# Moving ScalarE's K and V copies behind the second score's exps in a decoder block on one Trainium2 core

## The chip, the cores and the metric

The kernel runs on one core of a Trainium2 chip. The metric is device time in microseconds (us), the median of several executions; lower is better. Engines are called as in the profile: PE (matmul) with its weight loads PEld, DVE (VectorE), ACT (ScalarE), POOL (GpSimd), SP (which only issues DMAs here).

## What is computed

A decoder layer with three residual steps, each followed by a layer norm: linear attention over x (32 batches of 56 tokens, width 128, 16 heads), cross attention of x to a context of 1500 keys per batch, and a small feed-forward. Cut to what matters here, the cross attention:

```
qh = heads(q @ Wq.T + bq)          # 16 heads of 8
kh = heads(k @ Wk.T + bk)          # k = v = ctx, (32, 1500, 128)
vh = heads(v @ Wv.T + bv)
scores = einsum('bhqd,bhkd->bhqk', qh, kh) / sqrt(8)
attn = softmax(scores, axis=-1)
out = einsum('bhqk,bhkd->bhqd', attn, vh)
return concat(out) @ Wo.T + bo
```

## The kernel before

A front part does the linear attention and the queries of all 32 batches, a last part the feed-forward. Between them, from about 131 to 704 us, lies the main loop over batches, unrolled by two: `u` = 0 and 1. Each engine has its own written order of work; semaphores join them.

**Scores.** A batch has 12 scores of 125 keys (`KT`). Score t is 8 matmuls (line 1066) into two of three PSUM banks used in turn (`scores`). ACT turns each bank into probabilities with one `exp` activation (line 756), so a score has a pair of exps. PE may begin score t once the first exp of score t-1 is done. The products of probabilities and values, `pv`, are 32 short matmuls each time two scores are taken up (lines 1083 and 1089); they come two scores late.

**Steps and units.** A batch is six steps m of two scores. Between the scores PE does units of work for batches b+1 and b+2, in the order that `PLAN` writes out by hand:

```
PLAN = ((("M1", "M1", "M1", "K2"), ("M1", "M1"), ()),
        (("M1", "M1", "V"), ("M1", "M1"), ("T",)),
        (("M1", "K2", "M1", "M1"), (), ("M1", "M1")),
        (("K2", "Z"), (), ("X",)),
        (("M2", "V"), ("M2", "M2"), ("Y",)),
        (("M2", "M2", "V", "M2", "M2"), (), ()))
```

Each step has three parts, called one, two and three in the code. PE's order within a step is score 2m, part one, score 2m+1, part two, the `pv` of two earlier scores, part three. K2 (a third of the key projection of batch b+2, three matmuls, line 954) and V (a third of the values of batch b+1, twelve short matmuls, line 962) are copied out by ACT (`k_copy`, line 776, and `v_copy`, line 765). The M units (line 974) are a pass of scores from which DVE takes row maxima (line 1313); M1 is for batch b+1, M2 for b+2. X turns the maxima over and ACT copies them to `mT` (`m_copy`, line 771), which SP then brings into `q_diag` with four DMAs. T, Z and Y finish the output of a pair of batches and come in u=0 alone; DVE takes them up.

**The ring.** Every unit takes the next of four PSUM banks (`ring`), in the order of `PLAN`; a unit waits in `release` until the unit four places earlier has been taken out by its engine, through `DONE` (`k32_done` and `v_done` for K and V). Certain M units go as pairs (`PAIRS`): PE waits for the banks of both before the first. Counting units of u=0 from zero, K2's first (3) shares a bank with an M of step 1 (7), V's first (8) with an M of step 2 (12), K2's second (13) with the last M of step 2 (17), K2's third (18) with V's second (22), this with an M of step 5 (26), and V's third (28) with the second M of the next batch's step 0. Round u=1 is 28 units long and turned by three banks: V's first shares with K2's second, K2's third with an M of step 4's part two, the others follow as in u=0. I write K0, K1, K2 and V0, V1, V2 for the three units and copies of a batch, N0 to N6 for its M2 units.

**Other queues.** POOL splits the context in two halves, casts each copied K third to `kh` (line 580) and takes the rest `kl`; SP stores both halves and loads them back, stacked, as `k_stack` (line 439). SP's order in a batch is: load `k_stack`, place the maxima, load context, store K halves.

Of the kernel before, what the change touches and what calls it, by code (L numbers as in the profile page):

```python
# [241 lines left out]
def decoder_block(nc, ctx_dram, x_dram, pack_dram, out_dram, m):  # L242
# [6 lines left out]
    with ExitStack() as stack:  # L249
# [124 lines left out]
        with nc.Block() as block:  # L374
# [330 lines left out]
            def _(act):  # L705
# [44 lines left out]
                def exp(b, t):  # L750
                    for half in range(2):
                        k = 2 * t + half
                        act.wait_ge(s_ready, b * 2 * KT + k + 1)
                        if half == 0:
                            wait_past(act, pv_done, b * KT + t - PBUF + 1)
                        nc.scalar.activation(probs[0:KP, t % PBUF, half * 2 * GC:(half + 1) * 2 * GC],  # L756
                                             scores[k % RING_AT][0:KP, 0:2 * GC], ACT.Exp, scale=SCALE).then_inc(p_ready, 1)

                def v_copy(n, i, u, bank):
                    act.wait_ge(ready["V"], n * 3 + i + 1)  # L760
                    if i == 0:
                        wait_past(act, pv_done, (n - 1) * KT)
                    at = 4 * i * G * VW + 8
                    to = v_ext[u][0:KP, at:at + 4 * G * VW].rearrange("p (x a c) -> p x a c", a=2, c=VW // 2)
                    nc.scalar.copy(to[:, :, :, 0:2 * HD],  # L765
                                   bank[0:KP, :].rearrange("p (x a c) -> p x a c", a=2, c=2 * HD)).then_inc(v_done, 1)

                def m_copy(n, bank):
                    act.wait_ge(ready["X"], n + 1)
                    wait_past(act, m_placed, n * 64)  # L770
                    nc.scalar.copy(mT[:, :], bank.bitcast(F16)[0:MB, 0:P]).then_inc(m_ready, 1)  # L771

                def k_copy(n, i, bank):
                    act.wait_ge(ready["K"], n * KC + i + 1)
                    wait_past(act, kl_done, (n - 1) * KC + i + 1)
                    nc.scalar.activation(k32[:, i * CH:(i + 1) * CH], bank[:, 0:CH], ACT.Identity,  # L776
                                         bias=w("bk")).then_inc(k32_done, 1)
# [28 lines left out]
                def body(b, u, s1, s2):  # L806

                    def copies(units):
                        for kind, i in units:
                            bank = ring[slots[u][kind, i]]  # L810
                            if kind == "V" and s2:
                                v_copy(b + 1, i, 1 - u, bank)
                            if kind == "X" and s2:
                                m_copy(b + 1, bank)
                            if kind == "K1" and s2:
                                k_copy(b + 1, i, bank)
                            if kind == "K2" and s1:
                                k_copy(b + 2, i, bank)

                    for m, (one, two, three) in enumerate(plans[u]):  # L820
                        exp(b, 2 * m)
                        if not s2 and 2 * m in X2T_STEPS:
                            x2_T(X2T_STEPS.index(2 * m))
                        copies(one)
                        exp(b, 2 * m + 1)
                        copies(two + three)

                def x2_T(q):
                    act.wait_ge(x2T_ps, q + 1)
                    nc.scalar.copy(x2T[:, q, :], X2T_BANK).then_inc(x2T_sb, 1)  # L830

                for b in range(2):
                    body(b, b % 2, True, True)
                with act.Fori(1, B // 2 - 1) as i:
                    for u in range(2):
                        body(i * 2 + u, u, True, True)
                body(B - 2, 0, False, True)
                body(B - 1, 1, False, False)

# [705 lines left out]
```

## Time and profile before

| what | us |
|---|---|
| median of three runs | 758.32 |
| lowest and highest | 755.79 and 760.76 |
| profiled execution, its own time | 758.05 |
| span of that execution in the trace | 756.3 |

The profiled execution is one more run of the same program, with the hardware profiler on; its mean granted TensorE clock is 0.965 of full speed. All durations come from it. Times of rows count from the start of its span.

### The profile page before, as it was taken

To read this page: it belongs to the slowest core of one execution; us is meant where nothing else is said; L and a number is where in the kernel's file an instruction comes from. 1 tells how busy PE (TensorE), PEld (TensorE's weight loads), DVE (VectorE), ACT (ScalarE), POOL (GpSimd) and SP (SyncE) were. 2 spreads that over 40 slices of the span, in tenths; PEclk is the share of its full clock that TensorE was granted. 3 is DMA by queue.
4 is the path that set the end of the run, shared out by engine and by line. 5 is a ranking of instruction groups with operands and counts; after the bars stand their busy time and mean duration, and the time that the engine had idled before them with its cause. 6 is when DMAs were issued, how large, how long until landed. Compare 5 with 4: busy or idle time off the path is not lost.

```text
span 756.3 us, 33186 instructions
## 1 busy us (share of the span) xinstructions
PE 677.2 (90%) x12468; PEld 436.8 (58%) x12468; DVE 585.3 (77%) x1139; ACT 549.2 (73%) x1123; POOL 471.1 (62%) x507
## 2 busy tenths in 40 slices
PE   6779864989799999999999999999999999997883
PEld 3456431555566666666666666666666666665552
DVE  5768966766678888888888878888888788884597
ACT  4537523876678888888888888888888888887751
POOL 6525524574657677777777677767777767623464
PEclk9989976999999999999999999999999999999997
DMA  7203503587667777877788877778777778760001
GB/s 215 82 2 101 87 15 83 80 187 139 128 136 142 144 156 156 174 158 147 147 158 150 153 148 152 147 143 154 156 168 166 148 142 161 132 108 11 1 1 49
DMA packets 39405, 93.20 MB, mean 123 GB/s; under 512 B 7880, under 2 KB 14536, under 8 KB 39368
## 3 DMA queue, kind: packets, MB, share of 16 engines
q1 hardware_dynamic: 39368, 92.69, 60.6%
q8 instruction: 25, 0.41, 0.3%
q14 instruction: 12, 0.10, 0.1%
HBM read 66.06 MB, written 26.54 MB: 122 GB/s over the span
## 4 chain that ended last, share of the span: by engine, by line
PE 65%; DVE 14%; issue 9%; ACT 7%; DMA 2%; SPq 1%; POOL 1%; ACTq 0%; DVEq 0%; POOLq 0%
PE psum L974 13%; PE psum L1066 12%; PE psum L1083 11%; PE psum L962 9%; PE psum L1089 8%; DVE mx L1313 4%; ACT probs L756 4%; PE psum L954 3%; PE psum L905 2%; DMA q_diag<-mT 1%; PE psum L891 1%; DVE rden L1241 1%; PE psum L982 1%; DVE k_stack L1452 1%; DVE kf L1210 1%
## 5 line engine op out<-in xcount | busy, mean ns | idle before, releaser
L1313 DVE TENSOR_REDUCE mx<-psum 128x1 f32<-128x500 f32 x672 | 422.1, 673 | 103.3 <-PE psum L974 100.1
L756 ACT ACTIVATE probs<-psum 125x448 f32<-125x448 f32 x768 | 376.3, 544 | 88.8 <-PE psum L1066 85.2
L974 PE MATMUL psum<-kh,q_max 64*128 64x500 f16 (+1 forms) x672 | 148.6, 383 | 12.4 <-DVE mx L1313 11.2
L1066 PE MATMUL psum<-q_diag,k_stack 64*128 64x112 f16 x3072 | 143.0, 212 | 11.3 <-ACT probs L756 2.6
L1083 PE MATMUL psum<-probs,v_ext 125*32 125x112 f32 x3072 | 149.8, 266 | 2.0 <-issue 2.0
L1089 PE MATMUL psum<-probs,v_ext 125*32 125x112 f32 x3072 | 145.3, 261 | 0.0
L580 POOL CAST kh<-k 128x500 f16<-128x500 f32 x96 | 57.7, 601 | 134.5 <-ACT k L776 126.7
L1066 PEld LDWEIGHTS psum<-q_diag,k_stack 64*128 64x128 f16 x3072 | 90.3, 95 | 82.7 <-ACT probs L756 49.7
L568 POOL TENSOR_TENSOR c_hl<-c_in,c_hl 128x500 f16<-128x500 f32 x96 | 110.4, 1150 | 7.7
L586 POOL TENSOR_TENSOR kl<-k,kh 128x500 f16<-128x500 f32 x96 | 107.2, 1145 | 0.0
L1083 PEld LDWEIGHTS psum<-probs,v_ext 125*32 125x32 f32 x3072 | 74.3, 109 | 32.7 <-issue 23.7
L1089 PEld LDWEIGHTS psum<-probs,v_ext 125*32 125x32 f32 x3072 | 87.7, 111 | 0.0
L566 POOL CAST c_hl<-c_in 128x500 f16<-128x500 f32 x96 | 59.4, 619 | 38.9 <-PE psum L962 36.1
L962 PE MATMUL psum<-WvH,c_hl 128*128 128x128 f16 x768 | 76.7, 222 | 4.5 <-issue 4.5
L974 PEld LDWEIGHTS psum<-kh,q_max 64*128 64x128 f16 (+1 forms) x672 | 38.3, 94 | 69.7 <-DVE mx L1313 31.1
L962 PEld LDWEIGHTS psum<-WvH,c_hl 128*128 128x128 f16 x768 | 58.4, 99 | 24.9 <-DVE mx L1313 11.4
L776 ACT ACTIVATE k<-psum,pack 128x500 f32<-128x500 f32 x96 | 65.1, 679 | 9.6 <-PE psum L954 8.2
L962 PE MATMUL psum<-WvL,c_hl 128*128 128x128 f16 x384 | 70.4, 221 | 0.0
L765 ACT COPY v_ext<-psum 125x512 f32<-125x512 f32 x96 | 56.4, 588 | 5.9 <-PE psum L962 5.8
L954 PE MATMUL psum<-c_hl,WkH 128*128 128x500 f16 x192 | 57.2, 380 | 0.3 <-ACT mT L771 0.3
L607 POOL TENSOR_TENSOR q_max<-qh,pack 128x896 f16<-128x896 f32 (+1 forms) x32 | 54.1, 1689 | 1.4 <-ACT qh L747 1.4
L726 ACT ACTIVATE e_buf<-psum 128x512 f32<-128x512 f32 x32 | 19.6, 614 | 28.9 <-PE psum L891 25.9
(143 smaller groups left out, 698.5 us busy)
## 6 DMA issues: line engine op xcount, KB each, us to landing
k_stack<-k_halves SPq DMA_DIRECT2D x192, 187.5 KB, 6.3
c_in<-ctx_in SPq DMA_DIRECT2D x32, 750.0 KB, 5.5
k_halves<-kh SPq DMA_DIRECT2D x32, 375.0 KB, 6.0
k_halves<-kl SPq DMA_DIRECT2D x32, 375.0 KB, 6.4
q_stack<-q_halves SPq DMA_DIRECT2D x32, 64.0 KB, 2.5
q_diag<-mT SPq DMA_DIRECT2D x64, 0.8 KB
q_diag<-mT SPq DMA_DIRECT2D x64, 0.1 KB
out<-x_all SPq DMA_DIRECT2D x8, 112.0 KB
```

Source lines behind the costliest of these rows:

```text
L566: nc.gpsimd.tensor_copy(c_hl[:, buf, 0, keys], c_in[:, buf, keys]).then_inc(c_hi, 1)
L568: nc.gpsimd.tensor_tensor(c_hl[:, buf, 1, keys], c_in[:, buf, keys], c_hl[:, buf, 0, keys], ALU.subtract).then_inc(c_split, 1)
L586: nc.gpsimd.tensor_tensor(kl[u][:, keys], k32[:, keys], kh[u][:, keys], ALU.subtract).then_inc(kl_done, 1)
L756: nc.scalar.activation(probs[0:KP, t % PBUF, half * 2 * GC:(half + 1) * 2 * GC], scores[k % RING_AT][0:KP, 0:2 * GC], ACT.Exp, scale=SCALE ...
L776: nc.scalar.activation(k32[:, i * CH:(i + 1) * CH], bank[:, 0:CH], ACT.Identity, bias=w("bk")).then_inc(k32_done, 1)
L954: last = nc.tensor.matmul(bank[:, 0:CH], wt[:, :], c_hl[:, u, part, i * CH:(i + 1) * CH], start=(k == 0), stop=(k == 2))
L962: last = nc.tensor.matmul(bank[:, j * P:(j + 1) * P], c_hl[:, u, part, at:at + P], wt[:, :], start=(k == 0), stop=(k == 2))
L974: last = nc.tensor.matmul(bank[:, 0:CH], q_max[u][rows, r * P:(r + 1) * P], kh[u][rows, c * CH:(c + 1) * CH], start=True, stop=True)
L1066: mm = nc.tensor.matmul(scores[(2 * t + half) % RING_AT][:, g * PAIR:(g + 1) * PAIR], k_stack[u][rows, g, t * KP:t * KP + P], q_diag[u][ro ...
L1083: nc.tensor.matmul(O[32 * j:32 * j + 32, 0:2 * N], v_ext[u][0:KP, v:v + 32], probs[0:KP, t % PBUF, at:at + 2 * N], start=(t == 0), stop=(t ...
L1089: last = nc.tensor.matmul(O[32 * j:32 * j + 32, 2 * N:GC], v_ext[u][0:KP, v:v + 32], probs[0:KP, t % PBUF, at + 2 * N:at + GC], start=Fals ...
L1313: dve.tensor_reduce(mx[:, r * KC + c:r * KC + c + 1], bank[:, 0:CH], AX.X, ALU.max).then_inc(mx_done, 1)
```

## The change

In ACT's body of a batch, the copies of a step's part one (K and V units) are done behind the exps of score 2m+1 in place of ahead of them, together with those of parts two and three. Part one holds all six K and V copies of a batch; the copy of `mT` is in part three. No other engine's program is changed.

```diff
                         exp(b, 2 * m)
                         if not s2 and 2 * m in X2T_STEPS:
                             x2_T(X2T_STEPS.index(2 * m))
-                        copies(one)
                         exp(b, 2 * m + 1)
-                        copies(two + three)
+                        copies(one + two + three)
```

## Rows read from the trace of the kernel before

**Rows 1.** The page, part 1: busy us, share of the span, instructions.

```profile
PE 677.2 (90%) x12468; PEld 436.8 (58%) x12468; DVE 585.3 (77%) x1139; ACT 549.2 (73%) x1123; POOL 471.1 (62%) x507
```

**Rows 2.** The page, part 4: the chain of waits, shares by engine.

```profile
PE 65%; DVE 14%; issue 9%; ACT 7%; DMA 2%; SPq 1%; POOL 1%; ACTq 0%; DVEq 0%; POOLq 0%
```

**Rows 3.** Two batches: length; busy PE, PEld, DVE, ACT, POOL; granted clock; DMA share; GB/s.

```profile
388.55:423.69 35.14, 34.51 (x717) 22.47 (x717) 28.59 (x54) 29.50 (x63) 25.35 (x29) 1.00 0.79 154
```

**Rows 4.** The page, part 5: the exps (busy, mean ns, idle before).

```profile
L756 ACT ACTIVATE probs<-psum 125x448 f32<-125x448 f32 x768 | 376.3, 544 | 88.8 <-PE psum L1066 85.2
```

**Rows 5.** Timeline of ACT: start, length, what, [idle before it and its releaser].

```profile
397.28 0.97 ACT L756 ACTIVATE probs<-psum 125x448 f32<-125x448 f32 x2
398.63 0.98 ACT L756 ACTIVATE probs<-psum 125x448 f32<-125x448 f32 x2 [0.38 <-PE psum L1066]
399.50 0.68 ACT L776 ACTIVATE k<-psum,pack 128x500 f32<-128x500 f32 x1
400.05 0.99 ACT L756 ACTIVATE probs<-psum 125x448 f32<-125x448 f32 x2
400.90 0.24 ACT L771 COPY mT<-psum 7x128 f16<-7x128 f16 x1
401.15 0.98 ACT L756 ACTIVATE probs<-psum 125x448 f32<-125x448 f32 x2
402.09 0.58 ACT L765 COPY v_ext<-psum 125x512 f32<-125x512 f32 x1
402.57 0.99 ACT L756 ACTIVATE probs<-psum 125x448 f32<-125x448 f32 x2
...
405.87 0.98 ACT L756 ACTIVATE probs<-psum 125x448 f32<-125x448 f32 x2
...
422.85 0.98 ACT L756 ACTIVATE probs<-psum 125x448 f32<-125x448 f32 x2
```

**Rows 6.** Timeline of PE's weight loads: scores (L1066) and M units (L974).

```profile
397.93 0.10 PEld L974 LDWEIGHTS psum<-kh,q_max 64*128 64x128 f16 x2 [0.17 <-issue]
...
399.30 0.21 PEld L1066 LDWEIGHTS psum<-q_diag,k_stack 64*128 64x128 f16 x8 [0.27 <-ACT probs L756]
...
400.66 0.21 PEld L1066 LDWEIGHTS psum<-q_diag,k_stack 64*128 64x128 f16 x8 [0.27 <-ACT probs L756]
...
401.98 0.21 PEld L1066 LDWEIGHTS psum<-q_diag,k_stack 64*128 64x128 f16 x8
...
403.98 0.10 PEld L974 LDWEIGHTS psum<-kh,q_max 64*128 64x128 f16 x2
...
406.75 0.10 PEld L974 LDWEIGHTS psum<-kh,q_max 64*128 64x128 f16 x2
...
408.05 0.21 PEld L1066 LDWEIGHTS psum<-q_diag,k_stack 64*128 64x128 f16 x8 [0.41 <-ACT probs L756]
...
409.98 0.10 PEld L974 LDWEIGHTS psum<-kh,q_max 64*128 64x128 f16 x2
...
419.31 0.21 PEld L1066 LDWEIGHTS psum<-q_diag,k_stack 64*128 64x128 f16 x8
...
420.89 0.10 PEld L974 LDWEIGHTS psum<-kh,q_max 64*128 64x128 f16 x2
...
423.69 0.22 PEld L1066 LDWEIGHTS psum<-q_diag,k_stack 64*128 64x128 f16 x8 [0.29 <-ACT probs L756]
424.00 0.10 PEld L974 LDWEIGHTS psum<-kh,q_max 64*128 64x128 f16 x2
```

**Rows 7.** Timeline of SP: the issue of the six k_stack loads.

```profile
411.59 2.67 SPq L439 DMA_DIRECT2D k_stack<-k_halves  x6
```

**Rows 8.** The page, part 6: DMA issues, KB each, median us to landing.

```profile
k_stack<-k_halves SPq DMA_DIRECT2D x192, 187.5 KB, 6.3
```

**Rows 9.** Windows around a stop of PE early in the loop; columns as rows 3.

```profile
203.00:207.00 4.00, 1.28 (x23) 0.93 (x19) 0.68 (x1) 1.19 (x4) 3.28 (x4) 1.00 0.07 8
207.00:212.00 5.00, 5.00 (x86) 3.59 (x90) 2.92 (x5) 3.15 (x7) 0.40 (x1) 0.66 0.89 249
```

## Prediction

> **What bounds the kernel now.** I read the page's busy shares first, then the chain of waits, then a window over two consecutive batches of the main loop, and last the timelines of ACT and of PE's weight loads in that window. By busy time three engines look full: PE 90%, DVE 77%, ACT 73% [rows 1]. The reader should see that no single share settles anything here. The chain of waits gives PE 65% of the span and ACT 7% [rows 2]: most of the time the next thing that counts is the next instruction of PE, in PE's own order. In the two batches from 388.55 to 423.69, 17.57 us each, ACT is busy 29.50 of 35.14 us (84%) and DVE 28.59 (81%) [rows 3]. So PE sets the pace while ACT and DVE run close behind; whatever makes PE wait for either of them is paid in full, until PE meets a wait that would have lasted as long anyway.
>
> PE waits for ACT in two ways. A score waits for the exps three score banks back. And every projection, K or V unit lies in one of four ring banks, so the unit four places later in the written order can't begin before ACT has copied that bank out (release in unit). The change delays all those copies, so the second kind of wait is what has to be priced.
>
> **Constants from the rows.** One exp lasts 0.54 [rows 4]. From a score's first weight load to its first exp: 400.66 to 401.15, 0.49. From that first exp to the next score it lets through: 400.05 to 400.66, 0.61, that is one exp and 0.07 of signalling. From the first exp of a pair to the next ACT operation that waits for nothing: 398.63 to 399.50, 0.87. From a K copy's start to the exps behind it: 399.50 to 400.05, 0.55; the copy itself lasts 0.68. A V copy lasts 0.58 (402.09) and the one of mT holds ACT from 400.90 to 401.15, 0.25 [rows 5, 6].
>
> **The change, part by part.** No instruction is added or removed and no transfer is changed. Per batch six copies (three K, three V) go from between the exps of score 2m and those of score 2m+1 to behind the latter. A copy then begins 0.87 after the first exp of score 2m+1, which begins 0.49 after that score, and its bank is free 0.07 after its end. Counted from the weight load of score 2m+1, a V bank is free after 0.49 + 0.87 + 0.58 + 0.07 = 2.01, a K bank after 2.11. The question for each is when PE wants that bank. I call the batches by their ring order, u=0 (from 388.55) and u=1 (the next).
>
> Step 2, K1's copy, is wanted soonest: units 13 and 17 share a bank, and 17 is the second of the M pair at the end of the same step (both banks of a pair are awaited ahead of its first). The exps of score 5 begin at 397.28 [rows 5], so the copy would run from 398.15 to 398.83 and free the bank at 398.90. PE begins that pair at 397.93 [rows 6]. PE stands 0.97 longer. This is the surest term, since nothing else of PE can pass.
>
> Step 3 gives something back. K2's copy now stands ahead of score 7's exps: they begin at 400.05, although score 7 began at 399.30 and could have had them at 399.79. The next score waits for these exps (400.66, marked with ACT as releaser). Gain 0.26.
>
> Step 4 loses again. Behind score 7's exps, at e, now come K2's copy (e+0.87) and the one of mT (e+1.42), so the exps of score 8 begin at e+1.67 in place of e+0.61+0.49, and score 9, which needs the first of them, begins at e+1.67+0.61 = e+2.28. Before, it came 1.32 behind score 8 (400.66 to 401.98), at e+1.93. Loss 0.35.
>
> Step 5, V1's copy: bank free 2.01 after score 9. The pair that takes it (N3 and N4, the M units of batch b+2) came 2.00 after score 9 in u=0 (401.98 to 403.98): loss 0.01. In u=1 there is no Y unit ahead and it came 1.58 after (419.31 to 420.89): loss 0.43. Mean 0.22.
>
> Step 0 of the next batch, V2's copy: score 11's exps begin at 405.87, so the bank is free at 405.87 + 0.87 + 0.58 + 0.07 = 407.39; the first pair of the next batch began at 406.75, loss 0.64. From u=1 to u=0: 422.85 + 1.52 = 424.37 against 424.00, loss 0.37 [rows 5, 6]. Mean 0.51.
>
> Step 1, K0's copy: free 2.11 after score 1; PE wanted it 1.93 after (408.05 to 409.98). Loss 0.18. V0's bank is wanted only behind score 4, in u=1 by the second unit there; I put it at nothing, and a tenth of a us late in one batch of two would cost 1.5 in all.
>
> Sum per batch: 0.97 - 0.26 + 0.35 + 0.22 + 0.51 + 0.18 = 1.97. The terms add because each stall lies on PE, moves every later score by the same amount, and the next copy is counted from the next score. Batches 0 to 29 have all six copies with users behind them: 30 x 1.97 = 59. The profiled run took 758.05 (span 756.3, so 1.75 lies around it) and the median is 758.32, 0.27 above: 758.3 + 59 = 817.
>
> **What else the moved copies carry.** K2's copy feeds POOL's cast and subtraction, then SP's store and the load of k_stack. It moves from 399.50 to 399.79 + 0.97 + 0.87 = 401.63, by 2.13. The load was issued at 411.59 over 2.67 [rows 7] and lands after a median of 6.3 [rows 8], at 420.6; 2.1 later it is 422.7, and its user, the first score of the next batch but one, stood at 423.69 before it was itself moved [rows 6]. Covered. The copy of mT is not moved in the code, but is queued behind K2's: it comes at 402.18 instead of 400.90 [rows 5]. SP then issues four transfers into q_diag that the next batch's first score needs. From the mT copy to that batch's first pair there were 5.85; with the pair moved by 0.97 - 0.26 + 0.35 + 0.01 = 1.07, 5.64 are left. When these transfers land isn't in the rows, so this costs between nothing and 0.2 per batch, 0 to 6 in all. I take nothing, as score 12 waited for no transfer in this window. POOL's own queue only waits longer ahead of its casts; what is behind them is not wanted by PE for several us.
>
> Bounds of the rest: the signalling of a copy is not shown by itself; between 0 and 0.2 in place of 0.07 it is -0.07 to +0.13 on five terms, -10 to +20 at most. The gain of 0.26 may fail if X, which lies ahead of score 8 on PE, comes late: +8.
>
> **A rule of the Trainium skill against this.** In the window PE's matmul rows are busy 34.51 of 35.14 us but its weight loads only 22.47, 64%, below ACT's 84% [rows 3]. The Trainium skill (Perfetto Trace Analysis, Identifying the Most-Contended Engine) says that matmul busy time is a poor measure because matmuls are pipelined, and to judge PE by the share of weight loads and other engines by occupancy. By that rule ACT would be the most contended engine, its work is unchanged, and the time would stay near 758. The chain of waits [rows 2] speaks against it: PE's slack is inside the latencies of its order, not free to take a wait.
>
> **The rivals.** (a) Part of the stalls is covered: only those with large margins, K1's and V2's, count, and the small ones dissolve in waits for DVE that PE has anyway. 0.97 - 0.26 + 0.51 = 1.22, times 30: 37, so 795. For it: the four small terms are differences of a few tenths between rows. (b) Nothing moves, 758: ACT has the same work and is the busiest of those measured by occupancy, PE takes the waits up in its gaps. The 0.97 speaks against it. (c) Faster: the exps of every second score come earlier and the freed chain in step 3 counts alone: 30 x 0.26 = 8 less, 750. It decides if each bank is free before its next user, that is if the pair at 397.93 could start without K1's copy; the order of the ring banks says no. (d) The clock falls. Where PE did 1.28 us of work in 4 us (203 to 207), the granted clock in the next 5 us was 0.66, so part of it at the lower level of 1.2 GHz [rows 9]. If one stop per batch did this, up to 0.34 x 5 = 1.7 per batch, 51 in all, would come on top: 868. It needs stops like that one; mine are at most 1 us, and the clock in the window is 1.00 [rows 3].
>
> **How the numbers follow.** The forecast, 817, has 0.72; (a) 0.13; (b) 0.05; (c) 0.04; (d) 0.06. The range goes from 790, which takes in (a), to 835, the sum with most of its upper bounds; (b), (c) and (d) are left out. The runs before spread by 0.7%, so about 1% is what can be told from no change. Faster by over 1% is most of (c), 0.03; within 1% is (b) and the rest of (c), 0.06; slower 0.91.
>
> **What would show it.** In the changed kernel, per pair of batches: about 39 us in place of 35.14; the pair at the end of step 2 waiting for ACT's K copy by nearly 1 us; waits of PE for K and V copies (lines 776 and 765) that hardly exist now; score 8 close behind score 7's exps; PE's busy share down by some 5 to 10 points at a granted clock of 1.00. I am wrong if the M pairs start ahead of the copies' ends, if DVE's reduces take over as what PE waits for, or if exps begin later than 0.49 behind their score in odd scores.

## The result and the profile after

The changed kernel takes 813.62 us (median of four runs, 809.68 to 817.84) against 759.54 for the kernel before in the same series: ratio 1.072, 95% interval 1.068 to 1.077. The profiled execution took 817.24 with a span of 815.4. The forecast was 817 in a range of 790 to 835.

The page of the changed kernel, part 1 (busy us, share of the span, instructions) and the chain of waits:

```profile
PE 695.7 (85%) x12468; PEld 446.1 (55%) x12468; DVE 587.3 (72%) x1139; ACT 549.5 (67%) x1123; POOL 471.2 (58%) x507
...
PE 59%; ACT 14%; DVE 13%; issue 11%; ACTq 1%; DMA 1%; POOL 1%; DVEq 0%; POOLq 0%
```

ACT's and DVE's busy times are those of before [rows 1], and the numbers of instructions are those of before, so no engine was given more work. But ACT has gone from 7% to 14% of the chain [rows 2]. The same pair of batches as a window of the changed kernel (columns as rows 3):

```profile
417.29:456.43 39.14, 35.44 (x717) 22.94 (x718) 28.78 (x54) 29.54 (x63) 25.35 (x29) 1.00 0.70 138
```

It is 39.14 long in place of 35.14 [rows 3]: 2.00 us per batch, with DVE, ACT and POOL as busy as before (PE's own busy time, 0.9 more, says little, as the ends of its matmuls are modelled) and the clock granted in full. The rhythm can be read without any model from the copies of the finished sums, which DVE makes once per batch. Each list below has the first copy, two copies that lie two batches apart, and the last. Before:

```profile
152.90 0.38 DVE L1351 COPY o_sb<-psum 128x224 f32<-128x224 f32 x1
392.27 0.38 DVE L1351 COPY o_sb<-psum 128x224 f32<-128x224 f32 x1
427.41 0.38 DVE L1351 COPY o_sb<-psum 128x224 f32<-128x224 f32 x1
705.68 0.39 DVE L1351 COPY o_sb<-psum 128x224 f32<-128x224 f32 x1 [8.81 <-PE psum L1089]
```

After:

```profile
161.19 0.38 DVE L1350 COPY o_sb<-psum 128x224 f32<-128x224 f32 x1
421.44 0.38 DVE L1350 COPY o_sb<-psum 128x224 f32<-128x224 f32 x1
460.57 0.38 DVE L1350 COPY o_sb<-psum 128x224 f32<-128x224 f32 x1
764.87 0.39 DVE L1350 COPY o_sb<-psum 128x224 f32<-128x224 f32 x1 [8.81 <-PE psum L1088]
```

From the first to the last of these copies there are 552.78 before and 603.68 after: 50.9 more. In between, the pairs of batches repeat to within 0.02 in most of the middle twelve, so this period is the sharpest measure of an experiment here, sharper than the medians. The other 8.3 of the 59.1 between the two spans lie ahead of the first copy. Of these, 4.4 lie ahead of the loop, in code that the change does not touch: its first score begins at 130.89 before, at 135.30 after, and anywhere from 130.18 to 135.69 in the twelve kernels of the experiments. So only some 54.8 of the 59.1 lie in the loop.

The weight loads of PE in the changed kernel, at the places of [rows 6] (start, length, tile, what ended the idle time before):

```profile
425.84 0.10 PEld L973 LDWEIGHTS psum<-kh,q_max 64*128 64x128 f16 x2 [0.41 <-issue]
...
428.20 0.10 PEld L973 LDWEIGHTS psum<-kh,q_max 64*128 64x128 f16 x2 [1.12 <-DVE mx L1312]
...
429.57 0.21 PEld L1065 LDWEIGHTS psum<-q_diag,k_stack 64*128 64x128 f16 x8 [0.27 <-ACT probs L756]
...
430.81 0.21 PEld L1065 LDWEIGHTS psum<-q_diag,k_stack 64*128 64x128 f16 x8 [0.16 <-ACT probs L756]
...
431.65 0.11 PEld L961 LDWEIGHTS psum<-WvH,c_hl 128*128 128x128 f16 x2 [0.44 <-ACT k L776]
...
432.43 0.21 PEld L1065 LDWEIGHTS psum<-q_diag,k_stack 64*128 64x128 f16 x8
...
434.49 0.12 PEld L973 LDWEIGHTS psum<-kh,q_max 64*128 64x128 f16 x2
...
438.02 0.12 PEld L973 LDWEIGHTS psum<-kh,q_max 64*128 64x128 f16 x2 [0.73 <-DVE mx L1312]
...
439.31 0.21 PEld L1065 LDWEIGHTS psum<-q_diag,k_stack 64*128 64x128 f16 x8 [0.41 <-issue]
...
441.47 0.10 PEld L973 LDWEIGHTS psum<-kh,q_max 64*128 64x128 f16 x2 [0.19 <-issue]
...
451.59 0.21 PEld L1065 LDWEIGHTS psum<-q_diag,k_stack 64*128 64x128 f16 x8 [0.20 <-ACT probs L756]
...
453.66 0.10 PEld L973 LDWEIGHTS psum<-kh,q_max 64*128 64x128 f16 x2 [0.44 <-DVE mx L1312]
...
457.16 0.10 PEld L973 LDWEIGHTS psum<-kh,q_max 64*128 64x128 f16 x2 [0.52 <-issue]
```

The line at 431.65 is V1. The pair ahead of K1's M pair, which rows 6 leave out, stood here in the kernel before:

```profile
396.52 0.10 PEld L974 LDWEIGHTS psum<-kh,q_max 64*128 64x128 f16 x2 [0.41 <-issue]
```

The matmuls of three of these M pairs tell who was waited for (the bracket of PE itself):

```profile
428.21 0.39 PE L973 MATMUL psum<-kh,q_max 64*128 64x500 f16 x2 [0.88 <-ACT k L776]
...
438.05 0.70 PE L973 MATMUL psum<-kh,q_max 64*128 64x500 f16 x3 [0.60 <-ACT v_ext L765]
...
453.67 0.39 PE L973 MATMUL psum<-kh,q_max 64*128 64x500 f16 x2 [0.28 <-ACT v_ext L765]
```

A reader should compare the two lists. The weight load at 428.20 is put down to DVE, its matmul at 428.21 to ACT's K copy. This pair waits for two banks, one that DVE empties and one that ACT empties. DVE had long been done with its one, at 425.99:

```profile
425.31 0.68 DVE L1312 TENSOR_REDUCE mx<-psum 128x1 f32<-128x500 f32 x1
```

The experiments below settle that the wait is for ACT.

ACT in steps 2 to 4 of the same batch (against [rows 5]):

```profile
426.53 0.98 ACT L756 ACTIVATE probs<-psum 125x448 f32<-125x448 f32 x2 [0.48 <-PE psum L1065]
427.40 0.68 ACT L776 ACTIVATE k<-psum,pack 128x500 f32<-128x500 f32 x1
428.90 0.98 ACT L756 ACTIVATE probs<-psum 125x448 f32<-125x448 f32 x2 [0.82 <-PE psum L1065]
430.05 0.98 ACT L756 ACTIVATE probs<-psum 125x448 f32<-125x448 f32 x2 [0.18 <-PE psum L1065]
430.92 0.68 ACT L776 ACTIVATE k<-psum,pack 128x500 f32<-128x500 f32 x1
431.48 0.24 ACT L771 COPY mT<-psum 7x128 f16<-7x128 f16 x1
431.62 0.95 ACT L756 ACTIVATE probs<-psum 125x448 f32<-125x448 f32 x2
```

K1's copy runs from 427.40, 0.87 behind the first exp, and ends at 428.08; the pair begins at 428.20. ACT then stands idle 0.82 for PE: each engine waits for the other in turn, in a loop that goes from score 5 over its exps and K1's copy to the M pair and the next score.

### The profile page after: what moved, and what is told of

The parts are those of the page before. It is cut to its first block, busy times and chain, and to the rows that moved or that the text cites. A ratio compares the mean times of both kernels' runs of the same rounds, so it can differ in the third digit from the quotient of the medians.

```text
span 815.4 us, 33186 instructions
## 1 busy us (share of the span) xinstructions
PE 695.7 (85%) x12468; PEld 446.1 (55%) x12468; DVE 587.3 (72%) x1139; ACT 549.5 (67%) x1123; POOL 471.2 (58%) x507
## 4 chain that ended last, share of the span: by engine, by line
PE 59%; ACT 14%; DVE 13%; issue 11%; ACTq 1%; DMA 1%; POOL 1%; DVEq 0%; POOLq 0%
PE psum L973 13%; PE psum L1065 10%; PE psum L961 9%; PE psum L1082 6%; ACT probs L756 6%; PE psum L953 5%; PE psum L1088 5%; DVE mx L1312 4%; ACT k L776 3%; ACT v_ext L765 3%; PE psum L904 1%; PE psum L890 1%; DVE rden L1240 1%; PE psum L981 1%; DVE k_stack L1451 1%
## 5 line engine op out<-in xcount | busy, mean ns | idle before, releaser
L973 PE MATMUL psum<-kh,q_max 64*128 64x500 f16 (+1 forms) x672 | 150.2, 386 | 58.1 <-ACT k L776 26.6
L973 PEld LDWEIGHTS psum<-kh,q_max 64*128 64x128 f16 (+1 forms) x672 | 39.4, 94 | 125.5 <-DVE mx L1312 72.1
L765 ACT COPY v_ext<-psum 125x512 f32<-125x512 f32 x96 | 57.0, 594 | 0.0
```

What stands on the lines that cost most here:

```text
L765: nc.scalar.copy(to[:, :, :, 0:2 * HD], bank[0:KP, :].rearrange("p (x a c) -> p x a c", a=2, c=2 * HD)).then_inc(v_done, 1)
L973: last = nc.tensor.matmul(bank[:, 0:CH], q_max[u][rows, r * P:(r + 1) * P], kh[u][rows, c * CH:(c + 1) * CH], start=True, stop=True)
```

## The experiments

All were profiled; most were also timed beside the kernel before. The period is that of a pair of batches in the middle of the loop, as above; the last column is half of what it exceeds 35.14 by. In two of the kernels the pairs differ a little in turn, and the period is their mean: 35.54 to 35.62 in "before, K1 written later", 36.69 to 36.77 in "before, K1 and V2 later". The ratio and its interval are worked out over the runs; the ratio is not the quotient of the two medians.

| run | median, us | before, us | ratio, 95% interval | period, us | over before, per batch |
|---|---|---|---|---|---|
| the change | 813.62 | 759.54 | 1.072 (1.068 to 1.077) | 39.14 | 2.00 |
| K copies only | 791.87 | 762.31 | 1.038 (1.030 to 1.046) | 37.46 | 1.16 |
| V copies only | 781.98 | 762.31 | 1.025 (1.019 to 1.031) | 36.83 | 0.85 |
| K1 only | 785.74 | 762.31 | 1.032 (1.024 to 1.040) | 37.06 | 0.96 |
| V0 only | 761.30 | 762.31 | 0.998 (0.994 to 1.002) | 35.16 | 0.01 |
| the change, K1 written later | 795.88 | 759.39 | 1.044 (1.035 to 1.052) | 37.67 | 1.27 |
| before, K1 written later | 766.83 | 759.39 | 1.007 (1.003 to 1.012) | 35.58 | 0.22 |
| the change, K1 and V2 later | 802.01 | 759.39 | 1.053 (1.045 to 1.061) | 37.90 | 1.38 |
| before, K1 and V2 later | 784.6 (one run) | 762.15 | - | 36.73 | 0.80 |
| K2 only | 759.85 | 759.39 | 0.999 (0.994 to 1.003) | 35.27 | 0.07 |
| K1 between the exps | 771.90 | 762.15 | 1.016 (1.008 to 1.024) | 36.17 | 0.52 |
| all six between the exps | 775.76 | 762.15 | 1.017 (1.012 to 1.023) | 36.39 | 0.63 |
| K0 only | 767.82 (one run) | 762.15 | - | 35.44 | 0.15 |

The theory is that of the prediction: PE stands until ACT has emptied the ring bank that its next unit wants. The rival is ACT's order by itself: a copy behind the exps puts off the next score's exps, and PE stands for those.

**K copies only, V copies only.** The copies of one kind go behind the second score's exps, as in:

```diff
-                        copies(one)
+                        copies([x for x in one if not (x[0] == "K2")])
                         exp(b, 2 * m + 1)
-                        copies(two + three)
+                        copies([x for x in one if x[0] == "K2"] + two + three)
```

> Only the three K copies go behind the second score's exps, the V copies stay ahead. Bank theory (PE stands until ACT has emptied the ring bank that the unit wants): the terms of K1 (0.95 per batch in the trace after the change), K0 (0.22) and of steps 3 and 4 (0.05) stay, 1.22 x 30 = 37 us over before. Rival, ACT's order (a copy behind the exps puts off the next score's exps, and PE stands for those): K and V copies take ACT about the same time (0.68 and 0.58), so half of the 54 to 59 us, 27 to 32, and in the trace PE waits for exps rather than for K copies.

> Only the three V copies go behind the second score's exps. Bank theory: V1's term (0.27 per batch) and V2's (0.57) stay, V0's bank is not missed: 0.84 x 30 = 25 us over before, and together with the run of the K copies alone the whole loss. Rival, ACT's order: 22 to 27 in all, spread evenly over the three V copies; V0's step would be as much longer as the others.

Measured by the period: 1.16 and 0.85 per batch, for 1.22 and 0.84 expected, and their sum 2.01 is the whole 2.00. The medians, 29.6 and 19.7 over before, missed the expected 37 and 25 on the low side, as most totals here do (see the factor 30 below); 29.6 even lies in the rival's 27 to 32, so for the K copies the medians speak for the rival and not for the theory. The waits in the stretch from 300 to 600 us part the two. With the V copies moved (who waits, for whom: us in total, times, longest):

```profile
PEld psum L1066 <- ACT probs L756: 18.9, 73, 0.5
...
PE psum L974 <- ACT v_ext L765: 9.9, 24, 0.6
```

In the kernel before the second line does not occur. Its 24 times are three per pair of batches in 300 us: V1's bank in one batch of the two, V2's in both, as the prediction has it (V1's other term was 0.01). PE's waits for exps became shorter, not longer (26.1 before in the same stretch).

**One copy at a time.** The same edit with a condition on the step: `m == 2` for K1, `m == 1` for V0, `m == 3` for K2, `m == 0` for K0.

> Only K1's copy (step 2) goes behind score 5's exps. Bank theory: the pair of M units that ends the step waits 0.95 per batch for it: 28 us over before, half of the whole loss from one of six copies. Rival, ACT's order: one copy of six, about 9 to 10 us; in the trace before, the exps of score 6 began only 0.38 after ACT had come free, so even less.

> Only V0's copy (step 1) goes behind score 3's exps; its bank is wanted by no unit before score 4. Bank theory: no change that can be told, -2 to +2 us. Rival, ACT's order: as much as any other V copy, 7 to 9 us over before.

> Only K2's copy (step 3) goes behind score 7's exps. It is the one place where the change gives something back: score 7's exps begin 0.3 earlier. Bank theory with the measured steps: score 8 gains 0.12 to 0.18, then the exps of score 8 and, in every other batch, V1's bank come later: +0.05 per batch net, between -4 and +5 us. If the exps' earlier start were worth its full 0.26 to 0.33 per batch and nothing behind it were late: 8 to 10 us faster.

> Only K0's copy (step 0) goes behind score 1's exps. Bank theory: the first pair of step 1 waits 0.14 to 0.22 per batch for it, 35.4 to 35.6 per pair of batches in place of 35.14. Rival, ACT's order: a sixth of the loss, 35.8.

K1's copy alone costs 0.96 per batch, nearly half of everything, and 23.4 by the medians (28 expected), where the rival gave 9 to 10. V0's, whose bank nobody wants for some time, costs 0.01. So a copy behind the exps costs nothing as such; its bank's next user makes the price. K2's, with both signs in it, costs 0.07 (0.05 expected): the earlier start of score 7's exps is not worth 8 to 10 us. Part of what it costs is again a bank: V1's weight loads and matmuls now wait for K2's copy, once per pair of batches, a wait that the list of the kernel before does not have (300 to 600 us):

```profile
PEld psum L962 <- ACT k L776: 3.5, 8, 0.4
...
PE psum L962 <- ACT k L776: 1.2, 8, 0.2
```

K0's costs 0.15, in the expected 0.14 to 0.22 by the trace; it was timed once, so only the period counts here. The three add up: 0.15 + 0.96 + 0.07 = 1.18 for the K copies, against 1.16 measured together. The waits with K1 alone moved, 300 to 600 us:

```profile
PEld psum L974 <- DVE mx L1313: 29.5, 57, 1.1
PEld psum L1066 <- ACT probs L756: 23.8, 80, 0.5
...
PE psum L974 <- ACT k L776: 15.0, 17, 0.9
```

A batch of this kernel takes 18.5 us, and in 300 us there are 17 waits of 0.9 for a K copy: one per batch. The first line, weight loads waiting for DVE, also grew (from 11.2), though DVE was not touched: that is the pair's misnamed half.

**The wait taken away by another order of units.** K1 is written behind the M units of step 2, so that its bank falls to a unit of step 3; in a second form V2 goes behind the M units of step 5. Each was run with the copies as changed and as before.

```diff
-        (("M1", "K2", "M1", "M1"), (), ("M1", "M1")),
+        (("M1", "M1", "M1", "K2"), (), ("M1", "M1")),
...
-        (("M2", "M2", "V", "M2", "M2"), (), ()))
+        (("M2", "M2", "M2", "M2", "V"), (), ()))
```

> The changed kernel with one more edit: in step 2 the unit K2 is written behind the three M1 units in place of behind the first, so that K1's bank is wanted by a unit of step 3 and no longer by the last M of step 2. ACT's order stays as changed. Bank theory: the 0.95 per batch of step 2 goes, 28 us less than the changed kernel, 26 to 31 over before. Rival, ACT's order: no difference from the changed kernel, 54 to 59 over before.

> Control for the run before: the same edit of the order of units in the kernel before, copies where they were. Bank theory: in the kernel before, K1's copy ended 0.55 ahead of the pair that wanted its bank, so there is nothing to win: -3 to +4 us, the loss from K1's copy beginning only as score 5 begins, which puts off score 5's exps by 0.1. If the order of units is itself worth a lot, the run before shows nothing about banks.

> As the run with K1 written later, and V2 written behind the four M2 units of step 5, so that its bank is wanted by K0 of the next batch in place of by the first pair of M units. Bank theory: V2's term (0.57 per batch) shrinks to nothing or 0.2, another 11 to 17 us off: 10 to 20 over before. Rival, ACT's order: still 54 to 59 over before.

> Control for the run with K1 and V2 written later: that order of units with the copies where they were before. Bank theory: the missed gain of that run was eaten by waits that the order itself brings (V2 waiting for DVE's reduces, K0 for POOL's cast), so they are here too: the order alone costs 1.3 to 1.9 us per pair of batches over before (36.5 to 37.1 in place of 35.14), and the moved copies add only some 0.8 to 1.4 to it, against 4.00 in the original order. If V2's term did not depend on the next user of its bank, the moved copies add 2.1 here as they do with K1 alone written later, so this order would stand at 35.8.

With K1 written later the changed kernel falls to 795.88; the gain was put at 28 and is 18 by the medians, and the 36.5 over before lie above the 26 to 31 expected. The order costs something by itself: the control, expected at -3 to +4 us, came out 7.4 slower than before, its period 35.58, 0.44 per pair above before. Against its own control the change costs 37.67 - 35.58 = 2.09 per pair in place of 4.00, less by 1.91: as much as K1's 0.96 twice. The rival, by which ACT's unchanged order would have kept the loss, falls here.

With V2 later as well the expectation failed outright: 802.01, slower than without, where 10 to 20 over before was expected. The waits of M matmuls for V copies (L973 for L765) had fallen from 10.0 us in 24 times to 2.0 in 7, but others stood in their place. In the changed kernel with both units later, 300 to 600 us:

```profile
PE psum L961 <- DVE mx L1312: 6.7, 15, 0.6
PEld psum L953 <- POOL c_hl L568: 4.7, 16, 0.4
```

V2 now waits for a bank that DVE has to empty, and K0 for POOL's split of the next context, which starts only when V2 is done. I had looked at the next user of the moved unit's bank and not at whose bank it takes, nor at who waits for the unit itself. The control confirmed it: this order costs 36.73 - 35.14 = 1.6 per pair with the copies where they were, and the moved copies add 37.90 - 36.73 = 1.17, both within what was written down ahead of it. So V2's term, 0.57 per batch, shrank by (2.09 - 1.17) / 2 = 0.46.

**Half the delay.** The copy stands between the two exps of the second score.

```diff
-                        copies(one)
-                        exp(b, 2 * m + 1)
+                        exp(b, 2 * m + 1, (0,))
+                        copies(one)
+                        exp(b, 2 * m + 1, (1,))
```

> Dose: as the run with K1's copy alone moved, but the copy stands between the two exps of score 5 and not behind both, so its bank is free one exp earlier (0.43 to 0.49). Bank theory: the stall at the end of step 2 falls from 0.95 to 0.46 to 0.52 per batch, 14 to 16 us over before, 36.1 per pair of batches. Rival, ACT's order: no less than with K1 moved behind both (24 us), since the second exp of score 5 is now late too.

> All six copies stand between the two exps of the second score. Bank theory: each bank is free 0.43 to 0.49 earlier than in the changed kernel, so K1 keeps 0.5 per batch, V2 0.1 to 0.2, K0 and V1 nothing to 0.05, steps 3 and 4 about 0.05: 0.65 to 0.8 per batch, 20 to 24 us over before, 36.4 to 36.8 per pair. Rival, ACT's order: about half of the changed kernel's loss in every step, 27 to 30 us.

K1's copy between the exps costs 0.52 per batch, in the expected 0.46 to 0.52. Its four runs lie between 762.55 and 777.40, too far apart for their median (9.8 over before, 14 to 16 expected) to decide anything. The matmuls that wait for it, first with K1 between the exps, then with K1 behind both:

```profile
414.61 0.39 PE L976 MATMUL psum<-kh,q_max 64*128 64x500 f16 x2 [0.45 <-ACT k L776]
```

```profile
413.44 0.39 PE L974 MATMUL psum<-kh,q_max 64*128 64x500 f16 x2 [0.89 <-ACT k L776]
```

One exp less ahead of the copy, 0.44 less of a wait: the stall follows the copy's end. All six between the exps cost 0.63 per batch, just under the expected 0.65 to 0.8, and 13.6 by the medians, under the 20 to 24. None of the twelve kernels beats the kernel before by more than can be told.

## Why the prediction was right, step by step

- **PE's order is the bound.** Right. Each stall on PE went into the period in full, and the pieces add (2.00 against 1.16 + 0.85). The rule of the Trainium skill weighed in the prediction (Perfetto Trace Analysis, Identifying the Most-Contended Engine) would have made ACT, unchanged in its work, the measure, and rival (b), 758, is out by 56 us. After the change that rule still names ACT (29.54 of 39.14, 75%) above PE's weight loads (22.94, 59%): high occupancy of ACT did not mean that ACT's position in the order was free, and the spare share of PE was not there to be used.
- **K1, 0.97.** Measured 0.96 alone. In the trace the M pair comes 428.20 - 425.84 = 2.36 behind the pair ahead of it, in place of 397.93 - 396.52 = 1.41, which is 0.95 later, and ACT's K copy is named for 0.88 of it. The signalling, assumed to take 0.07, took 0.12 here (428.08 to 428.20).
- **K0, 0.18.** In the trace 441.47 - 439.31 = 2.16 in place of 1.93 [rows 6], 0.23; alone 0.15.
- **Steps 3 and 4, -0.26 and +0.35.** The net, 0.09, is near what was measured (0.07 alone), but that is luck: both parts were too large, and the second has in part another cause. From score 7 to score 8 there are 430.81 - 429.57 = 1.24 in place of 1.36, a gain of 0.12: the exps begin 0.48 behind their score as foreseen (430.05), but the score they let through comes 0.76 behind them, not 0.61, for PE now has its `pv` and X to finish. I had taken ACT for the last wait there without looking for what is late next. Step 4 then loses 432.43 - 430.81 = 1.62 less 1.32, 0.30 in this batch, but not to the exps of score 8 as the prediction has it: score 9's row at 432.43 names no wait. V1, which PE does ahead of score 9, stood until 431.65 because its bank is the one that K2's copy empties, and that copy ended at 431.60 (430.92 + 0.68). The prediction never priced this user. In u=1, where V1 takes another bank, score 9 does wait for the exps (451.59), and the loss there is 451.59 - 450.20 = 1.39 less 419.31 - 418.02 = 1.29, only 0.10.
- **V1, 0.01 and 0.43.** 434.49 - 432.43 = 2.06 in place of 2.00, and 453.66 - 451.59 = 2.07 in place of 1.58: 0.06 and 0.49.
- **V2, 0.64 and 0.37.** 438.02 - 434.49 = 3.53 in place of 2.77, and 457.16 - 453.66 = 3.50 in place of 3.11: 0.76 and 0.39. V1 and V2 together give a mean of 0.85, as the run with the V copies alone.
- **V0, nothing.** 0.01 alone. The Trainium skill (PSUM — Partial Sum Buffer, Summary: rules for kernel authors) says "Evacuate promptly — 2 MiB is tight". That reason is space, which no run here tests; in time, one late copy costs 0.96 per batch and another nothing.
- **The sum per batch, 1.97.** Measured 2.00. **The factor 30** was the mis-sized one: 813.62 - 759.54 = 54.1 is 27 batches' worth. The twelve middle pairs give 47.5 of the 50.9 between the first and the last copy of the sums. The two pairs ahead of them, 42.01 and 39.55 long before, became 44.02 and 40.54, 3.0 longer in all and not 8. The last pair became only 0.4 longer and not 2: its first batch, 29, lost 2.1, but batch 30, which the sum took to be unchanged, became 1.7 shorter. The early batches have stops before the change too [rows 9], and their length differs from kernel to kernel (the first pair took 38 to 49 in the profiled executions), so whether a stall is hidden behind such a stop or the stops just fell otherwise is not settled. The medians of nine of the twelve experiments lie below 30 times their last column too; the reason is open too. That the profiled executions differ by 59.2, almost exactly the forecast, is luck: 4.4 of it lie ahead of the loop.
- **What the moved copies carry (DMAs, POOL).** No wait of the moved chain reached PE; the share of DMA in the chain of waits even fell from 2% to 1%. The 6 us allowed for it were not needed; of the 8 allowed for step 3 about half were.
- **The rivals.** (a), that small stalls dissolve, failed: they were there to a few hundredths, and alone, K0's gave 0.15 of a forecast 0.18. (c) needed each bank free ahead of its next user, and K1's was not. (d) did not come: with stops of up to 0.9 us twice and more in 39 us the granted clock of the window stayed at 1.00, that is 2.4 GHz.

## What to carry to other kernels

A copy out of a shared bank has two neighbours in time: the copying engine's own queue, and the next user of the bank. To price a move, take for every bank, and not only for those that look close, the end of its copy and the start of the unit that wants it next; the slack between them (0.55 us for K1, over 1 for V0) is all that can be moved for nothing, and where PE's order is the bound the rest is paid once per batch. When the remedy is another order of units, look at three things: who takes the bank afterwards, whose bank the unit takes, and who waits for the unit. In a loop with a steady period, measure the period in one trace; it showed differences of 0.1 us per pair of batches where the runs of one kernel spread by 8 and more.

## What the runs showed that I had not expected

The same wait is named differently in two rows of one trace: at 428.20 the weight load of the pair is put down to DVE for 1.12, its matmul at 428.21 to ACT for 0.88. Over 300 us the weight loads' waits for DVE rose from 11.2 to 29.5 in the kernel where only K1's copy was moved. And the steadiness: of twelve middle pairs of batches in the changed kernel none differs from 39.14 by more than 0.01, though five engines and all the DMA queues take part.
